# Weighing the values in pairs of key tiles: one item of eight products in TensorE's order, and the five engines' order tables drawn up anew

## What is computed

```python
h = x @ W + pe                                   # embedding, 8 x 1024 x 128
z = layernorm(h)
Q, K, V = heads(z @ Wq + bq), heads(z @ Wk + bk), heads(z @ Wv + bv)   # 8 heads of 16
attn = softmax((Q @ K.T + causal_mask) / sqrt(16))
h = h + (attn @ V) @ Wo + bo
f = layernorm(layernorm(h)) * ln_scale + ln_bias
h_shared, h_expert = swiglu(f @ shared_in_w.T), swiglu(f @ expert_in_w.T)
# a group of experts is chosen per token, in it the two best of four, with softmax weights comb
h = h + h_shared @ shared_out_w.T + sum_e comb[:, e] * (h_expert @ expert_out_weight[e].T) + biases
```

## Time and profile before

| | us |
|---|---|
| time, median of 3 runs (1023.4 to 1024.91) | 1024.57 |
| the profiled execution: its own time | 1023.86 |
| the profiled execution: span of the trace | 1022.1 |
| PE busy | 965.0 (94%) |
| DVE busy | 763.6 (75%) |
| ACT busy | 599.1 (59%) |
| POOL busy | 325.3 (32%) |

### The profile page before, as it was taken

The page is one execution under the profiler, slowest core; times in us unless marked ns, Lnnn a source line. Parts: engine busy times, 40 slices in busy tenths (PEclk is TensorE's granted clock), DMA queues, the critical chain, the costliest instruction groups (busy, mean ns, idle before and its releaser), DMA issues.

```text
span 1022.1 us, 17138 instructions
## 1 busy us (share of the span) xinstructions
PE 965.0 (94%) x5488; PEld 647.8 (63%) x5488; DVE 763.6 (75%) x2441; ACT 599.1 (59%) x1365; POOL 325.3 (32%) x469
## 2 busy tenths in 40 slices
PE   4699999999999999999999999999999999999976
PEld 3445565767667676776667666676667666565544
DVE  4588668895898868885898858987788858877143
ACT  3045655476664765567664776557654766546734
POOL 5014213224242234324242234323141243313224
PEclk9999999999999999999999999999999999999999
DMA  2310022002120021101220021100220020200000
GB/s 64 122 48 20 16 67 62 2 1 54 39 61 2 2 75 48 30 2 35 58 62 2 2 75 34 45 2 20 73 62 2 2 70 21 58 2 1 11 1 21
DMA packets 32520, 35.02 MB, mean 34 GB/s; under 512 B 8752, under 2 KB 18992, under 8 KB 32304
## 3 DMA queue, kind: packets, MB, share of 16 engines
q1 hardware_dynamic: 32144, 33.41, 12.5%
q10 hardware_dynamic: 288, 0.52, 0.1%
HBM read 4.02 MB, written 4.19 MB: 8 GB/s over the span
## 4 chain that ended last, share of the span: by engine, by line
PE 83%; DVE 8%; ACT 4%; issue 2%; POOL 1%; DMA 0%; ACTq 0%; POOLq 0%; DVEq 0%; SPq 0%
PE bank_p L585 15%; PE bank_s L559 14%; PE bank_w L603 13%; PE bank_f L684 6%; PE bank_f L685 6%; PE bank_f L686 6%; PE bank_f L505 3%; PE bank_m L650 3%; PE bank_f L507 3%; PE bank_f L506 3%; ACT pt L1033 2%; DVE mx_far L772 2%; PE bank_m L523 2%; PE bank_m L618 1%; PE bank_m L544 1%
## 5 line engine op out<-in xcount | busy, mean ns | idle before, releaser
L1033 ACT ACTIVATE pt<-bank_p 128x512 f32<-128x512 f32 (+3 forms) x768 | 352.6, 491 | 257.0 <-PE bank_p L585 252.4
L559 PE MATMUL bank_s<-k_stack,q_stack 112*128 112x512 f32 (+3 forms) x768 | 270.5, 385 | 8.2 <-DVE mx L776 4.9
L776 DVE CUSTOM_DVE_ANT_0 bank_s<-bank_s,causal 128x384 f32<-128x384 f32 (+3 forms) x512 | 244.7, 506 | 41.7 <-PE bank_s L559 36.0
L585 PE MATMUL bank_p<-q_stack,k_stack 128*128 128x512 f32 (+3 forms) x768 | 257.4, 377 | 9.9 <-ACT pt L1033 9.2
L559 PEld LDWEIGHTS bank_s<-k_stack,q_stack 112*128 112x128 f32 x768 | 144.8, 194 | 98.9 <-DVE mx L776 45.1
L1181 POOL TENSOR_SCALAR_AFFINE_SELECT pt<-pt 128x512 f32<-128x512 f32 x128 | 82.0, 641 | 389.9 <-ACT pt L1033 389.9
L585 PEld LDWEIGHTS bank_p<-q_stack,k_stack 128*128 128x128 f32 x768 | 139.3, 190 | 97.5 <-ACT pt L1033 65.5
L772 DVE TENSOR_REDUCE mx_far<-bank_s 128x1 f32<-128x512 f32 x256 | 166.4, 682 | 18.1 <-PE bank_s L559 16.9
L603 PE MATMUL bank_w<-pt,v 128*32 128x512 f32 (+3 forms) x1536 | 161.6, 498 | 0.5 <-POOL pt L1181 0.3
L684 PE MATMUL bank_f<-wex_h,hid_h 128*128 128x512 f32 x256 | 103.6, 404 | 2.2 <-DVE sel L940 1.4
L685 PE MATMUL bank_f<-wex_l,hid_h 128*128 128x512 f32 x256 | 101.3, 396 | 0.0
(11 more groups left out here) (127 smaller groups left out, 1298.0 us busy)
## 6 DMA issues: line engine op xcount, KB each, us to landing
q_stack<-qk_h SPq DMA_DIRECT2D x128, 64.0 KB, 2.2
k_stack<-qk_h SPq DMA_DIRECT2D x128, 64.0 KB, 2.3
q_stack<-qk_l SPq DMA_DIRECT2D x64, 64.0 KB, 2.2
k_stack<-qk_l SPq DMA_DIRECT2D x64, 64.0 KB, 2.3
out<-h SPq DMA_DIRECT2D x16, 256.0 KB, 2.7
x_sb<-x_t SPq DMA_DIRECT2D x16, 64.0 KB, 2.2
hid<-w_expert SPq DMA_DIRECT2D x1, 1024.0 KB, 5.5
pos_sb<-pos ACTq DMA_DIRECT2D x2, 256.0 KB, 3.7
```

Of the source, the lines that this page charges most:

```text
L559: nc.tensor.matmul(s_bank[s % 2][:, 0:cols], q_stack[0:STACK, half, hd, t % HT * P:(t % HT + 1) * P], k_stack[0:STACK, hd // 2, key_place( ...
L585: nc.tensor.matmul(p_bank[p % 2][:, q0:HALF], k_stack[:, hd // 2, key_place(i, kt // HT), kt % HT * P:(kt % HT + 1) * P], q_stack[:, half, ...
L776: nc.vector.tensor_tensor_reduce(src, src, causal[:, HALF - cols:HALF], 1.0, -3.0e38, ALU.add, ALU.max, mx[:, u, col:col + 1]).then_inc(s_ ...
L1033: nc.scalar.activation(pt[:, k % PT_SLOTS, j, q0:HALF], p_bank[p % 2][:, q0:HALF], ACT.Exp, scale=0.25).then_inc(exp_done, 1)
```

## The change

In `streams`, the stream of weighings holds only the odd steps. An item `("weigh", k)` now does the steps k - 1 and k, eight products behind each other. It waits first for everything that both need: the exponentials of step k (which stand behind those of k - 1), the mask of step k, the values, and at a unit's start the `take` of the unit before. `pv_done` still counts up once per step. The products, their columns and their order among themselves are the same, and `PT_SLOTS` stays 3. The middle of period -2 is another: the second half's `stat1` stands ahead of the first half's `ztl`, `turn ("turn", 0)` ahead of the second half's values. All fifteen strings of letters are new: each has 12 letters fewer per image that is weighed in it. Of the tables the diff shows one row.

```diff
@@ streams(n)
     weighing = []
-    for k in range(NP_):
+    for k in range(1, NP_, 2):
         weighing.append(("weigh", k))
         if k in UNIT_LAST:
             weighing.append(("take", UNIT_LAST.index(k)))
...
     if n == -2:
-        first = front(0) + front(1)
-        first.remove(("emb", 1))
-        first.insert(first.index(("turn1", 0)), ("emb", 1))
-        middle = first + [("turn", 0), ("turn", 1)]
+        middle = [("emb", 0), ("stat1", 0), ("emb", 1), ("turn1", 0), ("stat1", 1), ("ztl", 0), ("q", 0), ("k", 0), ("v", 0),
+                  ("turn1", 1), ("ztl", 1), ("q", 1), ("k", 1), ("turn", 0), ("v", 1), ("turn", 1)]
...
 WEAVE = {
     "pe": (
-        "spsmspspmspspmppssmspswsppwppssmppppmswspsmspsmfcspsmpmfspfswpfdsfpsfwmsspwppsfsmfpfppsfspwcwpsds"
+        "sspmssppmpspsdmspsmppsppsppspwscmppdsmspspsmsspfpssmmwssffssppfsspffpfsfsmppwmmfswfpspsmfpsspm"
...
@@ weigh(i, k) on PE
                 u, kt = PROBS[k]
                 g, half = UNITS[u]
-                q0 = first_column(k)
                 pe.wait_ge(exp_done, (i * NP_ + k + 1) * G4)
                 if k in DIAG:
                     pe.wait_ge(mask_done, i * len(DIAG) + DIAG.index(k) + 1)
-                if kt == HT * half and g == 0:
+                if kt - 1 == HT * half and g == 0:
                     pe.wait_ge(m_taken, after(i, "v", half))
-                if kt == 0 and i * NU + u:
+                if kt == 1 and i * NU + u:
                     pe.wait_ge(pv_taken, i * NU + u)
-                for j in range(G4):
-                    first = (g * G4 + j) * VC
-                    mm = nc.tensor.matmul(w_bank[VW * j:VW * (j + 1), q0:HALF], v[:, i % 2, kt, first:first + VW],
-                                          pt[:, k % PT_SLOTS, j, q0:HALF], start=(kt == 0),
-                                          stop=(kt == HT * (half + 1) - 1), tile_position=(0, VW * j))
-                mm.then_inc(pv_done, 1)
+                for n in (k - 1, k):
+                    u, kt = PROBS[n]
+                    q0 = first_column(n)
+                    for j in range(G4):
+                        first = (g * G4 + j) * VC
+                        mm = nc.tensor.matmul(w_bank[VW * j:VW * (j + 1), q0:HALF], v[:, i % 2, kt, first:first + VW],
+                                              pt[:, n % PT_SLOTS, j, q0:HALF], start=(kt == 0),
+                                              stop=(kt == HT * (half + 1) - 1), tile_position=(0, VW * j))
+                    mm.then_inc(pv_done, 1)
```

More of the change, by code:

```diff
@@ L130 @@
-        "pwpsmssmsppsmpppdfsdsmwwmmpffmpmfwwpmfmfpmwpfpfpfdmffmpmmspsmssfssmsdpppspwppsspcpsswpsmspsmssfs"
-        "fpssmsswspsppppdpmssdsmsfcwpppfsfdwcwpsssfpwpmwcdw"
+        "mmpmmpmmmpdpmmmspssdsssssmpsmpssppsssssppmpmsspsssdpsswsdpssdsppspmdspspsspssssppspspspspspsppss"
+        "pspspspmsdspspwpspwpwssspssssppsppssssssspspspsppsmsssssspsmssmpdpswsspppwmmsmpppppssmpsssmppsss"
+        "smmmsspfwpmmsspmmfpmmffmfmwfppfpfpmpffmmppdcpmmwwpmsswsspwsppsfmsssssfdspsssfdcssmcpswfpsdspwpps"
+        "fmspsfwsscpdmwdspmpssppspdmsffsspmdppp"
@@ L150 @@
+        "dpmmssspmssspspppspwpsswppssssmsssmspwmmpfssssmwsmpmmpsmpsspsspmwdpsfmsppmpppsssssfmppsspppmspsm"
+        "psfpfsspspmwpfspspmpspsfppsppsssmfpsspsmsswdppfpppfpswsmpfmswppssswcwfpswfpscmdsdssfspdpwpsdpmps"
+        "ppmmmmpspcsssppwmmsffdssspwpmppsdfpcdw"
     ),
@@ L169 @@
-        "fppwfmspspswffwdsmsmsscwcssdsd"
+        "spwpmdssspwmpssmpspspmsssppsssspppppmspmsssspssppmsdspsfsfpfmswfpmfspmswwssfmsppfpmsffpmmssfsmpp"
+        "sspmfppspwmcsfpfpsfwpmpmppmppwfspdcfmsppmdppmspppfsmspssfssspmfmppmsmpfwpppsfspmpcmsffppwsfdsmsf"
+        "pmsspspfssppsmmspfpmfpssswpfwsppcmpsmspmwfpdsfpppspwpmspppspssspsmsfpcmpmsppmppdcpsssspfpwsssppm"
+        "sspffscwsmfsscsdsm"
     ),
     "pool": (
-        "sppwsmfwfmpppmppswppsmsppfmspmpmppmsfsspppspwspfspsmfspsspwfpsfmpssmsspmpssppssppfmmssfppmsssppp"
@@ L176 @@
+        "pspsmsppsssfdmccdf"
     ),
     "sp": (
[L178 to L181 removed]
+        "smpssmmspsmsppsssmswmpswsspscspfsssssssssspfsppsppfpspppmmppwsswspmfsppspfpspspsmpwfsfwpppmspssp"
@@ L182 @@
+        "ppmswpmsmspmsssmpfssmpmffpwpmcppcfmpmssppfspspfwppsssmfpffspppfsssmmspsmpmpmssspspwffmmpppsmsspp"
+        "mwpfpppssmfpspdwpdcpfcpddwwmpsspsfmpfmfwppmspmssfspdmpmssssppmpsspmpmsmpssppspcffspcsdfpffmmfpfp"
+        "sspwffssspspmpcdfd"
     ),
```

95 lines of the change are left out of this document (39 added, 56 removed).

## The result

The changed kernel takes 1037.6 us (median; 1037.12 to 1038.05), where the kernel before takes 1024.6: a ratio of 1.013, with a 95% interval of 1.0116 to 1.0146. I had predicted 1008, with a range of 997 to 1021. It is slower by 13 us where I expected 16 us less.

A forecast was written before the change was run, and what follows sets the result against it. PE was taken to bound the kernel, except at the two ends. The sum 1023.9 - 17.0 - 3 + 4 = 1007.9 us, with 0.7 us for the median 1008.6, was taken as 1008, range 997 to 1021.

The forecast's parts named there:

- What bounds the kernel now: Middle periods: PE sets the time, idle 1.6 of 117.0 us, so what leaves its list shortens the kernel.
- Pairs: -17.0: Weighings on PE: 81 entries go at 0.21 us each, 17.0 us saved, 2.1 us per middle period.
- New waits and the longer block: +4: Around the pairs: waits for ACT and DVE together cost 0.5 us per image, 4 us in all, between 0 and 8.
- half is given back: Rival, chance 0.15: half of DVE's dry 4.0 us per image lands on the path, giving 1020 us.
- slower than before: Rival, chance 0.08: three slots hold ACT at every pair and PE then waits, giving 1034 us.
- The slots: Three slots of pt: ACT's step k + 2 waits until the pair is weighed; PE then waits 0.2 to 1.0 us per image.
- The start: -3: Start, 28.69 to 59 us: the new order lets DVE take scores earlier, saving 3 us, between 0 and 6.
- The end: 0: Last image: nothing gained beyond the entries; the last 47 us change by +-2 us.
- The clock: +-1.7: PE's half-clock stretches: each costs at most half its length, so one more or one less is +-1.7 us.
- What would show it: Middle period about 115.3 us; 116.5 or more with PE idle 3 us or more would mean waits replaced switches.

The follow-up runs named there:

- q: Kernel before, order and entries untouched, odd weighing steps leave out their last 120 columns: 1012.9 us (0.9896).
- a: Changed kernel, but the first part's tables and the start's middle as before, image 0 weighed in single steps: 1026.4 us (1.0022).
- s: Kernel before, in images 0 to 6 the single steps 10 and 17 moved in PE's order, none joined: 1033.6 us (1.0091).
- l: Kernel before, only the pairs of 256 and 128 columns joined, at the second step's place: 1033.0 us (1.0094).
- m: Kernel before, only the pairs of 512 and 384 columns joined, at the second step's place: 1047.2 us (1.0219).
- n: Kernel before, only the pairs of 512 and 512 columns joined, at the second step's place: 1054.3 us (1.0302).
- o: Kernel before, only steps 10 with 11 and 16 with 17 of an image joined, 16 pairs in all: 1036.8 us (1.0132).
- p: Changed kernel, in images 1 to 6 steps 8, 10, 16 and 18 weighed alone, three prob ahead of the pair's place: 1058.6 us (1.0351).
- e: Kernel before with its old tables, all pairs joined at the second step's place, at the latest ahead of prob(k + 2, 0): 1084.1 us (1.0605).
- f: Changed kernel with four slots of pt instead of three, low halves of the experts' output weights left out: 1039.0 us (1.0161).
- g: Pairs in the old order, as in e, with four slots of pt and the same weights left out: 1088.3 us (1.0638).
- b: Kernel before with only the first part's tables changed, image 0 in pairs, later periods in single steps: 1034.1 us (1.0111).
- h: Changed kernel with products that nobody reads added on PE among image 0's first 32 scores: 1034.5 us (1.0118).
- c: Kernel before with only the last part's tables changed and image 7 in pairs: 1023.7 us (1.0001).
- j: Changed kernel, images 1 to 6 in single steps again, each even step three prob ahead of the pair's place: 1137.8 us (1.1112).
- i: Kernel before with products that nobody reads added on PE among image 0's first 32 scores: 1023.9 us (1.0005).

## Why the prediction was wrong, point by point

**What bounds the kernel now** was the first step to fail. I read PE as the bound from 1.6 us of idle time in 117.0, so that what leaves its list shortens the kernel. In that same period the starts of all products but the weighings' lie 24.0 us further apart, in sum, than their columns take at 2.4 GHz, and 26.6 us in the changed kernel. Half of this is no waiting: 12.2 us (12.9 after) are behind products other than `score` and `prob`, mostly the same 0.02 us behind one of 512 columns or 0.06 behind a record of 128, time after time. Behind `score` and `prob` it is 11.8 us, and 13.7 after; of these some 9 and 11 us lie above the smallest spacing that is usual at their size. Those are small waits under products that are recorded as still running. They grew by 1.7 us behind scores and 0.2 behind `prob`. Run q puts the price on it: 0.57 us of the period for each 1 us taken from PE.

**Pairs: -17.0.** Right as an amount of PE's time: 18.9 us, 0.23 per entry; a pair of 512 and 384 columns is 1.64 us in the chain, one of 512 and 512 is 1.85, as written down beforehand.

```profile
393.11 1.85 PE bank_w L598 x16
400.06 1.64 PE bank_w L598 x16
```

The Trainium skill's TensorEngine Tiling, section Key Properties, states that a change of the tiling mode drains TensorE; a cost that fits it is in the trace, at 0.23 us instead of the 0.33 of my estimate from it and the Trainium skill's TensorE: Matmul & The Clock Gate, section Single matmul latency. No run shows that a drain is what it consists of. As a term of the sum, -17.0 was wrong. By q's rates (0.57 and 0.71), 18.9 us are worth 11 to 13 us at unchanged places, an estimate.

**New waits and the longer block: +4.** This is the term that was mis-sized most: in a the weighings take 17.3 us less and the time is 2 to 3 us longer, so the waits are about 20 us, where I put 4. I asked who waits for a block of 2 us, and not what the first step had been doing where it stood. It stood between two `prob`, or two scores, that would have waited for ACT or DVE in any case; there it cost half or less, as s shows for step 10. Joined to the second, it costs in full, and its old place shows the wait. In the old order that is 0.27 us for a short pair, 0.60 for 512 and 384, 0.96 for 512 and 512 (l, m, n), 7.1 us per image in all. Two single steps that are only moved cost 1.3 us (s) where two pairs cost 1.6 (o), and one that stands alone in the new order, three `prob` ahead, costs 0.8 us (p). So the place alone can cost this much, without any longer block. What share of a pair's cost is its length stays open; for the short pairs and those of 512 and 384 no step was moved without being joined. The new tables win these 7 us back in the middle (117.2 for 124.0 in e), down to the level of before and no further: 2.4 us saved, 2.4 + 0.2 lost. What the new tables lose was not taken apart by a run; that it is the same mechanism is read from the wider spacing behind scores and `prob`. The mechanism was nearest to my rival "half is given back" with 1020, but all of it is, and it is paid on ACT's banks as well as on DVE's. That the rival "slower than before" has the nearest time, 1034, is chance: it was worked out from the slots. The rule of the Trainium skill's TensorEngine Tiling, section PSUM Bottleneck, that tiling doesn't speed up what empties PSUM, I had named there and given too small a chance; the 0.46 us that PE waits for ACT ahead of `prob` in s agree with it.

**The waits ahead of a pair.** One piece of it I had not seen at all. The steps 12 and 13 stood next to each other in the kernel before, and m leaves them in their place, but in one item, whose waits for both steps stand ahead of the first product. That alone puts step 14 back by 0.80 us per image, a third of m's 2.40. Before, step 12 ran while the exponentials of step 13 were being finished:

```profile
350.88 1.71 PE L603 MATMUL bank_w<-pt,v 128*32 128x512 f32 x16
```

and in m PE waits for them first:

```profile
360.21 1.71 PE L631 MATMUL bank_w<-pt,v 128*32 128x512 f32 x16 [0.74 <-ACT pt L1061]
```

The new tables place the pairs far enough back that the changed kernel shows no such wait in its middle period. Pairs with each step's own wait inside were not tried.

**The slots.** Not a cause: f and g. ACT waits for them as I had feared, 1.6 us per period of the changed kernel, but off the path.

**The start: -3.** Wrong by 14 us, the wrong sign too: +11 (a, b). I had looked at 28.6 to 59 us, and there nothing changes: the maximum of the 32nd score, which I had put 3 us earlier, ends at 58.4 us for 58.9, that of the 33rd at 60.6 for 60.0, and DVE is busy 19.52 us for 19.64. The first scores come 0.5 us earlier, where I had said that they can't:

```profile
28.20 0.66 PE L552 MATMUL bank_s<-k_stack,q_stack 112*128 112x128 f32 x2 [5.07 <-DMA k_stack<-qk_h]
```

The price comes behind it, where I didn't look: the ninth exponential ends at 70.1 us for 65.4, the 25th at 87.8 for 78.6, while the maxima of the scores keep pace until the 41st (67.0 for 66.0). The order takes more scores ahead of the exponentials, at a stage where ACT has little else.

Of the 11 us, the clock holds 3 at the least (h). In b it is at half for 10.2 us more than before (66.8 to 70.2 and 83.9 to 90.7 us); at half of their length these cost at most 5.1 of its 10.5 us, an estimate. The ninth exponential of b is 3.1 us late before any pair is weighed, and only 0.9 of them can be the clock's. So a part of the loss is the order's alone. That the rest is this order of scores and exponentials too is read from the traces. No run changed it alone, nor the second half's statistics alone, so it is argued, not shown. Nor does a run show what makes e lose 5.3 us in the old first order; the places of its pairs, as in the middle, are the likely cause.

**The end: 0.** Right, but the 2.5 us that c's weighings take less don't show either.

**The clock: +-1.7.** Right as a rate: a stretch of 6.8 us put back one image by 2.7 us in l and 3.1 in e, a little under half its length. But such stretches come in larger numbers than I had allowed for. In the start of the changed kernel the half clock lasts 12.2 us longer and comes back for 6.8, and single runs of the kernel before lie between 1020.9 and 1026.2 us.

**What would show it.** The line that a period of 116.5 or more means new waits came true at 117.2, but with PE recorded as idle for 0.9 us, not for 3 or more, and with the sum of its loads' waits smaller than before (11.4 us for 13.3). The saving per entry stayed within its bounds of 0.16 to 0.24 us, the waits of the new tables did not stay under 1 us per period. The waits that the trace books for PE don't hold the loss; only the spacing of starts does.

No version here beats both kernels: c is the same as before within 0.1%. Whether tables for pairs exist that keep the 2.4 us per period stays open.

## What to carry to other kernels

Price an instruction by what the engines behind it gain when it goes, not by its own length: in a hand-woven order, fillers stand where the engine would wait anyway, and one of 1.1 us was worth 0.15 to 0.64 us there (o, s) and 1.2 us in another place (s). An engine that shows 99% busy is not proved to be the bound; shortening it a little in place, with part of the work left out, gives the rate (here 0.57) before any order is redrawn. In a newly drawn order look past the stretch that it was meant for, up to the first point where all engines depend on the same image.

## What the runs showed that I had not expected

- A change of one step's place shifts the records of every image by nearly the same amount: to 0.03 us at most steps, to 0.17 at steps 12, 20 and 22. Only where a stretch at half clock falls in does an image differ by more (2.7 us in l, 3.1 in e). Such shifts add up (7.28 for three runs, 7.09 for all in one).
- After waits of 2.4 us for a mask, PE ran at half clock for 3.4 or 6.8 us in ten of twelve cases of j (0.56 and 0.50 in the stretches behind two of them), so that part of what a wait costs falls behind it.
- In the start of the kernel before, ten us of full clock instead of half (i) gained nothing: 1.0005.
- ACT's 17.3 us of waits for a slot in the changed kernel could be taken away (f) without any gain.
